# Expert choice for four tiles at a time, its links put one by one between the statistics of the attention loop

## Chip, core, metric

One core of a Trainium2 chip. The metric is the device time of one execution in microseconds (us); of the kernel before there are three timed runs and one profiled execution. The engines are called as the profile calls them: PE (TensorE, with PEld for its weight loads), DVE (VectorE), ACT (ScalarE), POOL (GpSimd), SP (the DMA queue of SyncE).

## What is computed

A gated cross-attention block and a gated mixture of experts over 64 sequences of 64 tokens with 128 features: 4096 tokens, all float32.

```python
x = x + tanh(g_xattn) * attention(layernorm(x), ctx)     # 16 heads of 64, q and k normalised by head
h = layernorm(x)
logits = h @ Wg;  probs = softmax(logits)                # 8 experts
vals, idx = top_k(probs, 2);  weights = vals / (sum(vals) + 1e-9)
expert e: silu(h @ W1[e] + b1[e]) @ W2[e] + b2[e]        # hidden width 512, for its tokens only
x = x + tanh(g_ffn) * (weighted sum of the two experts + 0.1 * (silu(h @ Ws1 + bs1) @ Ws2 + bs2))
```

Of two experts with the same logit the one with the lower number counts as the first.

## The kernel before

The 4096 tokens are 32 tiles of 128 (one per partition). Each engine runs a program of its own, written out by hand, and the engines meet at semaphores; the order of a program is the order in which its engine works, and an instruction whose wait isn't over holds up all behind it.

**The attention loop.** `steps` runs s from -5 to 31. A step works on several tiles at once: projections of tile s+2 and s+3, scores and softmax of tile s, the attention output of tile s-1, its residual and second layer norm (s-2, s-3), and the expert logits of tile s-4, which `keep_logits` (L889) copies to `lg_all`. DVE's step (L990) is in this order: `sum_squares` of q, `scale` of k, `row_sums` and `row_inverses` of the softmax, `residual` (L823, which PE waits for before it transposes the second half of k), two more `scale` and the other `sum_squares`, `normalise` (L883), then the statistics: `token_statistics` (bn_stats L813, bn_aggr L817) and `second_statistics` (L830, L832); then `maximum` (L855, when PE has done the scores) and `less_maximum_of` (L862), which PE waits for before it computes the logits (L1319) and the values, and ACT before the exponentials of the softmax; at the end `route_ranks`, `keep_logits` and `route`.

**Expert choice.** The tiles are routed BT = 8 at a time, in NB = 4 batches. The choice is a chain of small DVE instructions, each of which needs the result of the one before: `after` makes each of them count up `f_step` and then waits for that count. In the loop batch b starts 11 steps behind its first tile (`ROUTE_LAG`); five steps of eight carry a piece of it at the end of DVE's step: `less_highest` and `first_choice` (6 instructions), `highest_of_rest` and `second_choice` (6), `take_ranks` and `place` (4), `denominators` (3), `weigh` (3). ACT adds two small exponentials. PE counts the chosen experts with `ranks` (L1324 and L1326, 1 + BT small matmuls), and `take_ranks` (L929, L931) adds the running counts, so that `place` (L937) gives each token two rows (`slot`) of the array `routed` in HBM. Batches 0 to 2 are routed in steps 11 to 15, 19 to 23 and 27 to 31. Batch 3 comes behind the loop.

**Scatter.** POOL writes each tile's rows to `routed` by two indirect DMAs (L704), in the loop for the tile SCATTER_LAG = 15 steps back, so that tiles 0 to 17 go out in the loop and 14 tiles behind it.

**Behind the loop.** The last tile's attention is finished between transposes of the normed tokens (`transpose_tokens`, L1342), DVE's `lo_part` (L976) and the shared expert of five groups of four tiles (`shared_hidden` L1358 to L1360, `shared_result` L1374, `shared_out` L1043 and L1045). DVE also routes batch 3, then computes from the counts the schedule of the experts' work (L1074 to L1116). SP waits for the schedule and for all scatters before it loads rows of `routed` (L365). Then 40 work items run through the experts (`row_transpose` L1463, `row_hidden` L1475 to L1477, `row_out` L1491, results scattered by POOL at L763). At the end three more groups of the shared expert run while the experts' results come back: `shared_out` for groups 5 to 7 (L1039) and `combine` (L1168, L1172), which adds the two weighted expert rows to the tokens of group g, once ACT has weighted the second of them (L590).

## Time and profile before

| | us |
|---|---|
| median of 3 timed runs | 600.97 (599.75 to 601.02) |
| the profiled execution, device time | 599.88 |
| its span, first to last instruction | 597.7 |
| PE busy in the span | 567.4 (95%) |
| DVE busy | 454.2 (76%) |
| ACT busy | 453.3 (76%) |
| POOL busy | 359.9 (60%) |

The rows further down are of the profiled execution; times in them count from the start of its span, which is 2.2 us shorter than its device time. "Busy" of PE is not PE at its peak, since matmuls are pipelined. A row by stretch gives the window, its length, each engine's busy us with its instructions, TensorE's granted clock (1.00 is full), the DMA share and GB/s. A timeline row gives start, duration, engine, line and operation, and in brackets how long the engine had been idle and who ended that.

### The profile page before, as it was taken

The numbers are of one execution on the slowest core, as the hardware profiler recorded it, in microseconds if no ns is written. First come the engines' busy times: TensorE is split into PE (matmuls) and PEld (weight loads), VectorE is DVE, ScalarE is ACT, GpSimd is POOL, SyncE is SP. The second block draws the span as 40 slices with busy tenths as digits, with TensorE's granted clock in tenths as the row PEclk, the third lists the DMA queues.
The fourth block names the chain that finished last, engine by engine and source line by source line (L and its number), as shares of the span: only waits on it lengthen the run. The fifth ranks groups of instructions, "written<-read, shape, count | busy, mean of one in ns | idle before, by whom it ended". The sixth has DMA issues, their size and how long they took to land.

```text
span 597.7 us, 21071 instructions
## 1 busy us (share of the span) xinstructions
PE 567.4 (95%) x7675; PEld 508.0 (85%) x7675; DVE 454.2 (76%) x1048; ACT 453.3 (76%) x991; POOL 359.9 (60%) x709
## 2 busy tenths in 40 slices
PE   6989999999999999999999999889989999999993
PEld 5868888888888888878888888678889999999983
DVE  4689889889898988998998899755766554555637
ACT  3689999999888999888999988666445565565574
POOL 2545656756557787777778866757716555555410
PEclk9999999999999999999999999999999999999997
DMA  6910100120100101110020000001312222222155
GB/s 216 334 42 3 36 4 21 37 83 3 54 3 13 49 25 39 43 32 11 22 64 12 21 13 10 20 29 42 125 51 77 85 74 77 86 76 65 45 223 212
DMA packets 22500, 37.07 MB, mean 62 GB/s; under 512 B 5136, under 2 KB 13072, under 8 KB 22272
## 3 DMA queue, kind: packets, MB, share of 16 engines
q1 hardware_dynamic: 17792, 26.81, 14.2%
q0 software_dynamic: 4320, 8.92, 4.2%
q8 instruction: 63, 1.03, 0.7%
q14 instruction: 37, 0.30, 0.2%
q10 hardware_dynamic: 288, 0.00, 0.0%
HBM read 22.71 MB, written 13.01 MB: 60 GB/s over the span
## 4 chain that ended last, share of the span: by engine, by line
PE 76%; DVE 13%; issue 5%; ACT 2%; POOL 2%; DMA 2%; ACTq 0%; DVEq 0%; SPq 0%; POOLq 0%
PE ps L1491 10%; PE ps L1237 8%; PE ps L1205 7%; PE ps L1293 7%; PE ps L1207 6%; PE ps L1206 6%; PE ps L1263 6%; PE ps L1246 5%; PE ps L1278 4%; PE ps L1475 3%; PE ps L1476 3%; PE ps L1477 3%; PE ps L1374 2%; DVE wide L847 2%; DVE sm L869 2%
## 5 line engine op out<-in xcount | busy, mean ns | idle before, releaser
L763 POOL DMA_INDIRECT results<-spo,xs_ix x71 | 69.1, 973 | 69.3 <-DVE spo L1161 59.6
L439 ACT ACTIVATE qk_T<-ps,lnw 128x512 f32<-128x512 f32 x128 | 96.9, 786 | 6.8 <-PE ps L1237 6.2
L847 DVE TENSOR_TENSOR wide<-ps,rstd 128x512 f32<-128x512 f32 x128 | 87.1, 680 | 5.0 <-POOL rstd L678 5.0
L1205 PE MATMUL ps<-w_hi,xc_hi 128*128 128x512 f32 x192 | 87.1, 454 | 3.9 <-DVE w_lo L783 2.8
L840 DVE TENSOR_REDUCE ss<-wide 128x16 f32<-128x1024 f32 x64 | 77.8, 1216 | 15.4 <-ACT wide L415 14.0
L1237 PE MATMUL ps<-ident,wide 128*128 128x128 f32 x512 | 78.4, 278 | 4.0 <-ACT row_T L491 2.5
L415 ACT ACTIVATE wide<-ps 128x512 f32<-128x512 f32 x128 | 76.1, 596 | 2.2 <-PE ps L1207 2.2
L1237 PEld LDWEIGHTS ps<-ident,wide 128*128 128x128 f32 x512 | 58.9, 144 | 20.5 <-ACT spo L469 6.5
L1207 PE MATMUL ps<-w_hi,xc_lo 128*128 128x512 f32 x192 | 76.2, 397 | 0.0
L704 POOL DMA_INDIRECT routed<-rows_all,slot x64 | 65.4, 1021 | 17.5 <-issue 16.3
L1206 PE MATMUL ps<-w_lo,xc_hi 128*128 128x512 f32 x192 | 75.6, 394 | 0.0
L572 ACT ACTIVATE qk_T<-ps,b_now 128x256 f32<-128x256 f32 (+1 forms) x160 | 59.7, 451 | 17.7 <-PE ps L1477 15.8
L1491 PE MATMUL ps<-w_sb,qk_T 128*128 x568 | 70.3, 276 | 0.0
L1491 PEld LDWEIGHTS ps<-w_sb,qk_T 128*128 128x128 f32 x568 | 66.9, 192 | 0.1
L684 POOL TENSOR_TENSOR prob<-prob,rinv 128x1024 f32<-128x1024 f32 x32 | 60.9, 1904 | 9.7 <-DVE rinv L876 9.6
L1293 PE MATMUL ps<-wu_sb,spo 128*128 128x128 f32 x512 | 62.5, 275 | 0.1
L1293 PEld LDWEIGHTS ps<-wu_sb,spo 128*128 128x128 f32 x512 | 59.8, 192 | 3.3 <-ACT qk_T L439 0.4
L855 DVE TENSOR_REDUCE mx<-ps 128x8 f32<-128x512 f32 x64 | 41.2, 686 | 16.9 <-PE ps L1263 16.9
L1161 DVE TENSOR_TENSOR spo<-ps,b_all 128x256 f32<-128x256 f32 (+1 forms) x40 | 15.8, 396 | 46.9 <-PE ps L1491 46.9
L469 ACT ACTIVATE spo<-ps 128x512 f32<-128x512 f32 x64 | 34.9, 596 | 20.0 <-PE ps L1278 20.0
L1475 PE MATMUL ps<-w_lo,w_hi 128*128 128x256 f32 (+1 forms) x160 | 47.8, 299 | 1.2 <-DVE w_lo L1124 1.2
L1477 PE MATMUL ps<-w_lo,w_hi 128*128 128x256 f32 (+1 forms) x160 | 44.9, 280 | 0.0
(202 smaller groups left out, 1354.3 us busy)
## 6 DMA issues: line engine op xcount, KB each, us to landing
v_sb<-routed SPq DMA_DIRECT2D x31, 130.0 KB
xc_in<-in_x SPq DMA_DIRECT2D x8, 256.0 KB, 2.9
xc_in<-in_ctx SPq DMA_DIRECT2D x8, 256.0 KB, 4.7
w_raw<-in_L_ffn_W SPq DMA_DIRECT2D x8, 256.0 KB, 2.7
out_x<-x_res SPq DMA_DIRECT2D x8, 256.0 KB, 2.0
x_res<-in_x SPq DMA_DIRECT2D x1, 1792.0 KB, 8.6
w_raw<-results SPq DMA_DIRECT2D x3, 512.0 KB, 4.6
rows_all<-results SPq DMA_DIRECT2D x3, 512.0 KB, 8.6
```

Of the source, the lines that this page charges most:

```text
L415: nc.scalar.activation(sq[:, n, j * 512:j * 512 + 512], ps[2 * n + j][:, :], ACT.Square, scale=HD ** -0.5).then_inc(sq_ready[n][j], 1)
L439: nc.scalar.activation(qk_T[:, n, 4 * j:4 * j + 4, :].rearrange("p a n -> p (a n)"), ps[6 + j][:, :], ACT.Identity, bias=lnw[:, 2 * n + 1: ...
L763: gp_.indirect_dma_start(out=results[:, :], out_offset=bass.IndirectOffsetOnAxis(ap=xs_ix[:, b4, a:a + 1], axis=0), in_=yb[:, b4, a, :], i ...
L840: nc.vector.tensor_reduce(ss[:, n, :], sq[:, n, :].rearrange("p (h d) -> p h d", h=HEADS), AX.X, ALU.add).then_inc(ss_ready[n], 1)
L847: nc.vector.tensor_tensor(qk_n[:, n, j * 512:(j + 1) * 512].rearrange("p (h d) -> p h d", h=8), ps[2 * n + j][:, :].rearrange("p (h d) -> ...
L1205: nc.tensor.matmul(out_bank, xc_hi[:, t % XD, src, :], w_hi[:, w, cols[j]], start=True, stop=False)
L1206: nc.tensor.matmul(out_bank, xc_hi[:, t % XD, src, :], w_lo[:, w, cols[j]], start=False, stop=False)
L1207: return nc.tensor.matmul(out_bank, xc_lo[:, t % XD, src, :], w_hi[:, w, cols[j]], start=False, stop=True)
L1237: last = nc.tensor.transpose(ps[6 + j][:, a * P:(a + 1) * P], qk_n[:, n, c0:c0 + P], ident[:, :])
L1293: last = nc.tensor.matmul(ps[7][:, 0:D], o_T[:, p, :, :].rearrange("p b n -> p (b n)"), wu_sb[:, p, :], start=(p == 0), stop=(p == PAIRS - 1))
L1475: nc.tensor.matmul(h, w_hi_c, xs_hi[:, n % 2, cols_n], start=True, stop=False)
L1491: last_ = nc.tensor.matmul(ps[4 + n % 2][:, a * D:(a + 1) * D], hT[:, n % 2, c, a * P:(a + 1) * P], w2e[:, c, :], start=(c == 0), stop=(c ...
```

## The change

- BT becomes 4, so there are 8 batches. Six of them (0 to 5) are routed in the loop, batch b in the four steps from 4b + 8 (`ROUTE_LAG` 8): there is a batch at work in every step from 8 to 31. Batches 6 and 7 come behind the loop.
- Each link of the chain is a function of its own, and the wait for the link before stands in front of it (`last`), no longer behind the link it follows. `choose(s, piece)` gives DVE five links a step, one at each of five places: in front of `token_sums`, between it and `token_moments`, behind that, between `second_sums` and `second_moments`, and behind that; `token_statistics` and `second_statistics` are cut in two for it. Nothing of the choice but `take_ranks` is left at the end of DVE's step. ACT's small exponentials come one step later in the batch than before.
- The weights of a batch (`inverse`, `first_weight`, `second_weight`) are computed in the next batch.
- Behind the loop DVE gets, between the work that it had there: `divide(5)`, `choose_first(6)` before `lo_part(0)`, `choose_second(6)` before `residual(30)`, `place(6)` behind `lo_part(1)`, `weigh(6)` before `residual(31)`; batch 7 stands where batch 3 stood. PE counts batch 6 between the two halves of `shared_hidden(0)`, and waits for `take_ranks(6)` before the logits of tile 29.
- SCATTER_LAG becomes 13: tiles 0 to 19 go out in the loop, 12 tiles behind it.
- `combine(0)` stands in front of `shared_out(5)`.

The core of the diff (left out: helpers of the same kind as those shown):

```diff
@@ -27,7 +27,7 @@
 GN = GT * P
 EARLY = 5
 ROW = D + 2
-BT = 8
+BT = 4
 NB = TILES // BT
 XD = 4
 RT = 256
...
@@ -235,8 +235,8 @@
         block = stack.enter_context(nc.Block())
 
         LAST = TILES - 1
-        SCATTER_LAG = 15
-        ROUTE_LAG = 11
+        SCATTER_LAG = 13
+        ROUTE_LAG = 8
         RANKS_AT = 2
         PADS_AT, SPARES_AT, SPARES_SENT_AT, SPARES_DONE_AT = 7, 8, 9, 15
 
@@ -264,7 +264,7 @@
 
         def batch_at(s, lag):
             b, at = divmod(s - lag, BT)
-            return (b, at) if 0 <= b < NB - 1 else (None, 0)
+            return (b, at) if 0 <= b < NB - 2 else (None, 0)
 
         def r_slot(n):
             return n % 4, 16 * (n // 4 + 1)
...
@@ -500,9 +500,9 @@
 
             def route(s, lag):
                 b, at = batch_at(s, lag)
-                if b is not None and at == 0:
+                if b is not None and at == 1:
                     expert_exponentials(b)
-                if b is not None and at == 1:
+                if b is not None and at == 2:
                     second_exponentials(b)
 
...
             hi_part(1)
+            expert_exponentials(NB - 2)
             probabilities(0, LAST)
             probabilities(1, LAST)
+            second_exponentials(NB - 2)
             sc.preload_act_table_set("silu_and_others")
...
-            def token_statistics(t):
+            def token_sums(t):
...
+
+            def token_moments(t):
+                if has(t):
                     ve.wait_ge(bn_done, t + 1)
...
-            def second_statistics(t):
+            def second_sums(t):
...
+            def second_moments(t):
+                if has(t):
                     ve.wait_ge(bn2_done, t + 1)
...
-            choice = [0]
-
-            def after(ins):
-                choice[0] += 1
+            links = [0]
+
+            def last():
+                ve.wait_ge(f_step, links[0])
+
+            def link_of(ins):
+                links[0] += 1
                 ins.then_inc(f_step, 1)
-                ve.wait_ge(f_step, choice[0])
 
             def by_expert(a):
                 return a.unsqueeze(2).to_broadcast([P, BT, E])
 
             first_of = first_e[:, :].unsqueeze(1).to_broadcast([P, BT, E])
+
+            def logits_of(b):
+                return lg_all[:, BT * b:BT * b + BT, :]
+
+            def first_at(b):
+                return rows_all[:, BT * b:BT * b + BT, D + 1]
+
+            def highest(b):
+                ve.wait_ge(lg_ready, BT * (b + 1))
+                link_of(nc.vector.tensor_reduce(gm, logits_of(b), AX.X, ALU.max))
+
             def less_highest(b):
-                ve.wait_ge(lg_ready, BT * (b + 1))
-                lg = lg_all[:, BT * b:BT * b + BT, :]
-                after(nc.vector.tensor_reduce(gm, lg, AX.X, ALU.max))
-                nc.vector.tensor_tensor(gp, lg, by_expert(gm), ALU.subtract).then_inc(f_sub, 1)
+                last()
+                nc.vector.tensor_tensor(gp, logits_of(b), by_expert(gm), ALU.subtract).then_inc(f_sub, 1)
+
+            def ties(b):
                 ve.wait_ge(f_sub, b + 1)
-                after(nc.vector.scalar_tensor_tensor(tie, gp, 0.0, first_of, ALU.is_equal, ALU.mult))
+                link_of(nc.vector.scalar_tensor_tensor(tie, gp, 0.0, first_of, ALU.is_equal, ALU.mult))
+
+            def first_expert(b):
+                last()
+                link_of(nc.vector.tensor_reduce(first_at(b), tie, AX.X, ALU.max))
 
...
+            def others(b):
+                last()
+                link_of(nc.vector.scalar_tensor_tensor(rest, oh[:, 0, :, :], -3.0e38, gp, ALU.mult, ALU.add))
 
             def highest_of_rest(b):
+                last()
                 nc.vector.tensor_reduce(top, rest, AX.X, ALU.max).then_inc(f_top, 1)
...
+            def both_choices(b):
+                last()
                 nc.vector.tensor_tensor(picked[:, 0:BT, :], oh[:, 0, :, :], oh[:, 1, :, :], ALU.add).then_inc(f_cnt, 1)
...
+            def hits(b):
                 ve.wait_ge(f_taken, 2 * b + 2)
-                after(nc.vector.tensor_tensor(hit, oh, rank.unsqueeze(1).to_broadcast([P, 2, BT, E]), ALU.mult))
+                link_of(nc.vector.tensor_tensor(hit, oh, rank.unsqueeze(1).to_broadcast([P, 2, BT, E]), ALU.mult))
+
+            def slots(b):
+                last()
                 with nc.allow_low_precision("slots are whole numbers"):
                     nc.vector.tensor_reduce(slot[:, b, :, :], hit, AX.X, ALU.add).then_inc(f_slot, 1)
 
...
+            def choose(s, piece):
+                b, at = batch_at(s, ROUTE_LAG)
                 if b is None:
                     return
                 if at == 0:
-                    less_highest(b)
-                    first_choice(b)
+                    if piece == 0:
+                        highest(b)
+                    if piece == 1:
+                        less_highest(b)
+                    if piece == 2:
+                        ties(b)
+                    if piece == 3:
+                        first_expert(b)
+                    if piece == 4:
+                        first_choice(b)
                 if at == 1:
-                    highest_of_rest(b)
-                    second_choice(b)
-                if at == RANKS_AT:
-                    place(b)
+                    if piece == 0:
+                        others(b)
+                    if piece == 1:
+                        highest_of_rest(b)
+                    if piece == 2:
+                        equal_of_rest(b)
+                    if piece == 3:
+                        ties_of_rest(b)
+                    if piece == 4:
+                        second_expert(b)
+                if at == 2:
+                    if piece == 0:
+                        second_choice(b)
+                    if piece == 1:
+                        both_choices(b)
+                    if piece == 2 and b >= 1:
+                        inverse(b - 1)
+                    if piece == 3 and b >= 1:
+                        first_weight(b - 1)
+                    if piece == 4 and b >= 1:
+                        second_weight(b - 1)
                 if at == 3:
-                    denominators(b)
-                if at == 4:
-                    weigh(b)
+                    if piece == 0:
+                        hits(b)
+                    if piece == 1:
+                        slots(b)
+                    if piece == 2:
+                        gate_sum(b)
+                    if piece == 3:
+                        denominator(b)
+                    if piece == 4:
+                        with_second(b)
...
-                token_statistics(s + 3)
-                second_statistics(s - 2)
+                choose(s, 0)
+                token_sums(s + 3)
+                choose(s, 1)
+                token_moments(s + 3)
+                choose(s, 2)
+                second_sums(s - 2)
+                choose(s, 3)
+                second_moments(s - 2)
+                choose(s, 4)
                 maximum(1, s)
                 maximum(0, s)
                 less_maximum_of(1, s)
@@ -1008,23 +1102,61 @@
                 less_maximum_of(0, s)
                 route_ranks(s, ROUTE_LAG)
                 keep_logits(s - 4)
-                route(s, ROUTE_LAG)
             steps(step)
...
+            def choose_first(b):
+                highest(b)
+                less_highest(b)
+                ties(b)
+                first_expert(b)
+                first_choice(b)
+                others(b)
+
+            def choose_second(b):
+                highest_of_rest(b)
+                equal_of_rest(b)
+                ties_of_rest(b)
+                second_expert(b)
+                second_choice(b)
+                both_choices(b)
+
+            def place(b):
+                take_ranks(b)
+                hits(b)
+                slots(b)
+
+            def divide(b):
+                inverse(b)
+                first_weight(b)
+                second_weight(b)
+
+            def weigh(b):
+                gate_sum(b)
+                denominator(b)
+                with_second(b)
+                divide(b)
+
             normalise(LAST - 2)
+            divide(NB - 3)
             row_sums(LAST)
             row_inverses(LAST)
+            choose_first(NB - 2)
             lo_part(0)
             keep_logits(LAST - 3)
+            choose_second(NB - 2)
             residual(LAST - 1)
-            second_statistics(LAST - 1)
+            second_sums(LAST - 1)
+            second_moments(LAST - 1)
             lo_part(1)
+            place(NB - 2)
             nc.vector.tensor_scalar(tg01[:, :], tg[:, 1:2], SHARED, None, ALU.mult).then_inc(run0, 1)
...
             normalise(LAST - 1)
+            weigh(NB - 2)
             residual(LAST)
-            second_statistics(LAST)
+            second_sums(LAST)
+            second_moments(LAST)
...
-            less_highest(NB - 1)
-            first_choice(NB - 1)
-            highest_of_rest(NB - 1)
-            second_choice(NB - 1)
+            choose_first(NB - 1)
+            choose_second(NB - 1)
             lo_part(2)
-            take_ranks(NB - 1)
             place(NB - 1)
             shared_out(0)
-            denominators(NB - 1)
             weigh(NB - 1)
...
+            combine(0)
             shared_out(EARLY)
-            combine(0)
...
+                    if t == LAST - 2:
+                        pe.wait_ge(f_taken, 2 * (NB - 1))
...
             shared_hidden(0, range(2))
+            ranks(NB - 2)
             attend(LAST)
```

## Rows read from the trace of the kernel before

**Rows 1.** Busy us of PE, PEld, DVE, ACT, POOL; stretches: steps 11-16, 17-18, 19-24, 27-29.
```profile
154.71:224.83 70.12, 68.98 (x1147) 59.12 (x1149) 64.09 (x138) 63.12 (x135) 48.22 (x110) 1.00 0.09 31
224.83:247.12 22.29, 22.29 (x383) 19.66 (x386) 19.88 (x40) 20.69 (x45) 17.70 (x39) 1.00 0.10 26
247.12:317.74 70.62, 69.19 (x1147) 59.35 (x1150) 64.01 (x138) 63.00 (x135) 53.36 (x115) 1.00 0.12 37
340.07:376.03 35.96, 34.27 (x577) 28.96 (x580) 32.72 (x73) 30.64 (x65) 25.04 (x55) 1.00 0.05 14
```

**Rows 2.** The chain of waits in step 19, where DVE hands back to PE.
```profile
256.16 0.28 DVE x_res L823
...
256.49 0.66 PE ps L1237 x4
```

**Rows 3.** Timeline of DVE and PE in step 17, a step without choice.
```profile
224.53 0.34 DVE L883 TENSOR_SCALAR rows_all<-x_res,mv,rstd 128x128 f32<-128x128 f32 x1
224.79 0.28 DVE L813 BATCH_NORM_STATS2 bn<-x_res 128x6 f32<-128x128 f32 x1
225.11 0.18 DVE L817 BATCH_NORM_AGGREGATE mv<-bn 128x2 f32<-128x6 f32 x1
225.99 1.29 DVE L855 TENSOR_REDUCE mx<-ps 128x8 f32<-128x512 f32 x2 [0.30 <-PE ps L1263]
227.20 0.68 DVE L862 TENSOR_TENSOR prob<-ps,mx 128x512 f32<-128x512 f32 x1
228.06 0.29 PE L1319 MATMUL ps<-wg_raw,row_T 128*128 128x8 f32 x2
232.22 0.32 DVE L823 SCALAR_TENSOR_TENSOR x_res<-ps,tg,x_res 128x128 f32<-128x128 f32 x1
233.12 0.60 PE L1237 MATMUL ps<-ident,wide 128*128 128x128 f32 x4
233.95 1.22 DVE L840 TENSOR_REDUCE ss<-wide 128x16 f32<-128x1024 f32 x1 [0.82 <-ACT wide L415]
```

**Rows 4.** The chain of waits in step 21: a gap, and PE's count.
```profile
273.65 0.36 issue
...
275.81 0.05 PE ps L1324
275.86 0.19 PE ps L1326 x8
```

**Rows 5.** Timeline of DVE in step 13: two instructions that need nothing of each other.
```profile
183.25 0.21 DVE L929 TENSOR_TENSOR w_raw<-ps,base 128x64 f32<-128x64 f32 x1
183.38 0.15 DVE L931 TENSOR_TENSOR base<-ps,base 128x8 f32<-128x8 f32 x1
```

**Rows 6.** Timeline behind the loop: batch 3's choice on DVE, and PE behind it.
```profile
407.22 0.22 DVE L905 TENSOR_REDUCE w_raw<-lg_all 128x8 f32<-128x64 f32 x1
...
410.33 0.68 DVE L976 TENSOR_TENSOR w_lo<-ps,w_lo 128x512 fp32r<-128x512 f32 x1
...
411.16 0.63 PE L1342 MATMUL ps<-ident,rows_all 128*128 128x128 f32 x4 [0.58 <-DVE w_lo L976]
```

**Rows 7.** Timeline behind the loop: the last tile's probabilities and residual 30.
```profile
393.33 0.25 DVE L876 RECIPROCAL rinv<-sm 128x16 f32<-128x16 f32 x1
...
394.69 0.34 DVE L823 SCALAR_TENSOR_TENSOR x_res<-ps,tg,x_res 128x128 f32<-128x128 f32 x1
...
395.71 1.07 PE L1246 MATMUL ps<-ident,prob 128*128 128x128 f32 x8 [0.24 <-POOL prob L684]
```

**Rows 8.** Timeline of POOL, SP and PE: the last batch's scatters, row loads, first expert matmul.
```profile
413.27 0.95 POOL L704 DMA_INDIRECT routed<-rows_all,slot  x1 [1.17 <-DVE slot L937]
...
436.07 13.47 SPq L365 DMA_DIRECT2D v_sb<-routed  x6
...
441.07 0.39 PE L1475 MATMUL ps<-w_lo,w_hi 128*128 128x256 f32 x1 [1.16 <-DVE w_lo L1124]
```

**Rows 9.** Timeline of DVE near the end: `shared_out` of group 6.
```profile
584.88 0.75 DVE L1039 SCALAR_TENSOR_TENSOR x_res<-ps,tg,x_res 128x512 f32<-128x512 f32 x1 [0.30 <-PE ps L1374]
```

49 lines of the change are left out of this document (29 added, 20 removed).

## The prediction

> **What bounds the kernel now.** I read the views in this order. The page's busy shares (PE 95%, the others 60 to 76%) say only where to look. The busy time by stretch says what a step costs and which steps differ. In steps 17 and 18, which carry no choice, PE is busy for all of the 22.29 us, at the full granted clock: a step is 11.15 us of PE's work, and DVE has 19.88 of 22.29 busy [rows 1]. The three stretches with choice are longer: steps 11 to 16 take 70.12 us where six plain ones take 66.87, steps 19 to 24 take 70.62 for 66.87, steps 27 to 29 take 35.96 for 33.44. That is 3.25 + 3.75 + 2.52 = 9.5 us of excess, with PE idle for 1.14, 1.43 and 1.69 us of it and stretched matmuls for the rest [rows 1]. The chain of waits says who does it: in step 19 it leaves PE, runs down DVE through the choice, and comes back only when `residual` has read the output (L823 to PE's transposes at L1237) [rows 2]. So in these steps DVE is the bound, in the others PE.
>
> The timeline of a plain step says how much room DVE has. It idles twice: 0.30 us in front of `maximum`, waiting for the scores, and 0.82 us before the second sum of squares, waiting for ACT [rows 3]. Between the two it runs without a pause, so a delay of `maximum` is passed on. PE would feel it at two points. The residual is through at 232.54 and PE transposes the second half of k at 233.12, 0.6 us of slack. The logits start at 228.06, when `less_maximum_of` ended at 227.88: some 0.1 us of slack, which is all there is [rows 3].
>
> **The loop, what goes.** In the old place, the end of DVE's step, the choice stands between `less_maximum_of` and `residual` and has only the residual's 0.6 us of slack to hide in. Six links take 1.56 us there: in the same form behind the loop 12 links run from 407.22 to 410.33, 0.26 us a link [rows 6]. So a step with six links has to be about 1 us longer, and six such steps are 6 of the 9.5. From the excess of 9.5 I take what the change doesn't touch. PE's count is 0.05 + 0.19 us for each of three batches [rows 4], 0.72. In step 21 there is a gap of 0.36 us on PE in which it waits for nothing that the profile shows, with slower matmuls behind it [rows 4]; I leave 0.6 for it. 9.5 - 0.7 - 0.6 = 8.2 us go, if the new place is free.
>
> **The loop, what comes.** Five links a step in steps 8 to 31, 24 steps. No row shows a link of four tiles; from both sides: the instructions on 64 elements take 0.21 to 0.23 us and those on 8 take 0.15 [rows 5, 6], so 32 elements take about 0.19. What a link costs DVE depends on whether it has to wait for its neighbour. The upper end is one that waits: 0.22 (0.19 and the 0.03 to 0.05 by which 0.26 exceeds 0.22). The lower end is one that doesn't: L931 starts 0.13 us behind L929, which takes 0.21 [rows 5], so the next instruction starts some 0.08 before the profile's end of the one before, and a link on 32 elements costs 0.10 to 0.11. The places are laid out so that neighbours are never links: I go through one step. `normalise` gives way after 0.26 (224.53 to 224.79). Link 0 at 0.26, `token_sums` at 0.36, link 1 at 0.56, `token_moments` at 0.68, because it waits for its sums 0.32 us either way (224.79 to 225.11, [rows 3]); link 1 lies in that wait and costs nothing. Link 2 at 0.78, `second_sums` at 0.88, link 3 at 1.08 in the second such wait, `second_moments` at 1.20, link 4 at 1.30, DVE free at 1.40. `maximum` now starts at 1.46 (225.99 - 224.53), for the scores. So the five links fit into the two waits and the 0.30. In the step with `hits` (64 elements) it is 1.45, and the two or three instructions on 4 elements in the other steps are shorter. The middle is zero a step; I book 0.02 us for it, 0.5 us in all, since a margin of 0.05 isn't a margin. Bounds: 0 and, with every link at 0.22, see the rival below.
>
> PE's count: 1 + 4 small matmuls for six batches. By 0.19/8 us each and 0.05 that is 0.15, six times 0.9, for 0.72 now: +0.2. Below nothing it can't go, as the instructions grow in number. `take_ranks` stays where it is, twice as often, two instructions of 0.13 and 0.08: 3 more times 0.2 us, in the slack of 0.6 and of 0.82. ACT's exponentials come in 12 steps, at 0.2 us; they now need nothing of the same step. ACT is busy 20.69 of 22.29 us in two steps [rows 1], and what it delays, DVE's next `scale`, stands in front of the 0.82 us [rows 3]. Cost nothing; with that cover gone it would be 0.2 us in 12 steps.
>
> POOL: four more scatters in the loop, in steps 13 and 14, where it is as little loaded as in the stretch's mean, 48.22 of 70.12 us busy [rows 1]. What is queued behind a scatter on POOL is the next tile's reciprocal root, and a tile's slots are ready two steps before its scatter. Nothing.
>
> **Behind the loop.** `divide(5)` takes the place of the three instructions of the old `weigh`, during ACT's exponential. Then it costs: `choose_first(6)` starts behind `row_inverses`, 0.17 us after 393.33. Six links at 0.22 are 1.3, then `lo_part(0)` 0.6, `keep_logits` 0.1, `choose_second(6)` 1.2, and the residual of tile 30 starts at about 396.6 in place of 394.69 and is through at 396.95. PE's transposes of the second half of the last probabilities wait for it; they stand in the group that starts at 395.71, whose second half comes at about 396.24, half of its 1.07 us later [rows 7]. PE is 0.7 us late, with PE's count of batch 6 0.85; with links at 0.26 it would be 1.3. `place(6)` and `weigh(6)` lie beside PE's shared expert. What comes back: batch 7's twelve links take 12 x 0.22 = 2.65 in place of 3.11 us, and PE now waits 0.58 us for the `lo_part` behind them [rows 6], so all of 0.45 counts, and the count is 0.1 shorter. 0.85 - 0.45 - 0.1 = +0.3 us, bounds -0.1 and +1.0.
>
> The scatters: 12 tiles in place of 14 are left over, four scatters fewer, and the 1.17 us that POOL waited for the slots of batch 3 goes, since batch 6 is placed early. Sixteen scatters and the landing lie between 413.27 and 436.07 [rows 8], 1.43 us each at most; so SP can load rows 5 to 7 us sooner. This buys nothing by itself: the rows are there, PE's first matmul of the experts at 441.07 waits for DVE's `row_lo` (L1124) [rows 8], which stands behind the last `shared_out` and `lo_part`, and these behind PE's shared expert. The rows' transposes are late by at most a microsecond less than that. If they were the bound after all, it would be a gain of up to 1 us.
>
> **Near the end.** `combine(0)` moves into time in which DVE waits for PE's group 5; DVE is then ready some 0.4 us sooner for `shared_out(6)`, and there it waits for PE already now, 0.30 us [rows 9]. The gain is eaten: 0. It could be negative if ACT's weighting were late; PE needs `shared_out(5)` only for group 7, microseconds later.
>
> **The sum,** against the profiled execution's 599.88 us (span 597.7 and 2.2 around it): -8.2 + 0.5 + 0.2 + 0.3 = -7.2, so 592.7. That execution lies 1.1 below the median of the runs, 600.97, from which the same sum gives 593.8. I say 593.3.
>
> **A rule against it.** L931 starts while L929, by the profile, has 0.08 us to go [rows 5], and on this the links at 0.10 us rest. The Trainium skill, VectorE: DVE Perf Modes, The DRAIN you can't avoid, states that the next DVE operation doesn't start until the pipe of the last is empty and that leaving the semaphore out saves nothing; its Rules for kernel authors say to minimise the number of operations, not of semaphores. By it some 60 more small instructions in the loop (six batches of 22 less three of them, for three of 22) each cost their whole duration, which is the first rival's mechanism and its 609. The trace disagrees with the rule's strong form, by 0.13 against 0.26 us.
>
> **Rivals.** (1) Slower: a link costs its full 0.22 us wherever it stands, because DVE starts it only when its neighbour is done. Five are 1.1 us in front of `maximum`; 0.30 of idle time and 0.1 of slack before PE's logits cover 0.4, and PE is 0.7 us late in each of 24 steps: +16.8. With -8.2 + 0.5 for count and tail that is +9.1, 609. It decides from 0.32 us a step, where 24 of them eat 7.7. For it: the margin is so narrow, and waits stand in front of nearly every link. Against it: rows 5. Chance 0.07. (2) The gaps are only half used: a link costs 0.13 and each one between sums and moments pushes these by 0.05, so that `maximum` is late by 0.15 to 0.3 and PE by 0.05 to 0.25 a step: 1.2 to 6 us back, 594.5 to 599, typically 596.5. Chance 0.22. (3) It doesn't do what it says, since the excess has another cause than the choice (PE's code, POOL's scatters from step 15 on): against it speaks that steps 17 and 18, with scatters, are plain [rows 1]; 600. Chance 0.04. (4) More: the gap of step 21 was the choice's too, DVE gains margin and the rows' loads counted: 590 to 591.5. Chance 0.07.
>
> **Numbers.** The forecast, 591.5 to 595, has 0.60. The range for 8 in 10 takes in the fourth and most of the second: 590.5 to 598.8. What this kernel's measurement can tell from no change is about 0.2%, 1.2 us. Faster than that: 0.60 + 0.07 + 0.21 = 0.88; within it 0.05; slower 0.07.
>
> **What the profile after would show.** Right: steps 8 to 29 all at 11.15 to 11.35 us with PE busy throughout; links in front of `maximum` 0.10 to 0.15 us apart from their neighbours, and `maximum` still waiting for PE, if for 0.05 us. Wrong: `maximum` starting with no idle time before it, PE idle before L1319 or the values. Behind the loop PE idle for 0.7 us before the last probabilities' second half, the scatters ending over 5 us ahead of the first row's work, and `shared_out(6)` waiting 0.7 us. It is wrong as a whole if plain steps become longer than 11.4 us.

## The result, and the profile after

The changed kernel takes 597.81 us (median, 595.34 to 599.53) where the kernel before takes 601.02 (599.75 to 602.15): a ratio of 0.9941, 95% interval 0.9925 to 0.9957. The forecast was 593.3 us, a gain of 7.7 with a range of 590.5 to 598.8; it gained 3.2. The profiled execution took 597.49 us (span 595.7) beside 599.88 (span 597.7) before. Tables below speak of the *tail*: from the start of the last tile's scores on PE to the first matmul of the experts. A *gap* is a stretch in which PE stands still though the profile shows nothing that it waits for ("issue").

The first view is busy time by stretch, for the same steps as [rows 1] (columns as there).

```profile
155.65:222.72 67.07, 67.07 (x1141) 59.13 (x1140) 62.12 (x147) 62.36 (x135) 52.47 (x114) 1.00 0.12 36
222.72:245.15 22.43, 22.43 (x385) 19.77 (x384) 20.81 (x51) 20.93 (x47) 17.76 (x39) 1.00 0.08 26
245.15:314.87 69.72, 67.58 (x1141) 59.51 (x1140) 62.48 (x147) 62.58 (x135) 53.38 (x115) 1.00 0.11 37
338.21:371.27 33.06, 32.93 (x565) 28.84 (x564) 30.49 (x70) 30.09 (x64) 25.10 (x55) 1.00 0.05 15
```

Steps 11 to 16 went from 70.12 to 67.07 us and steps 27 to 29 from 35.96 to 33.06, PE busy in all of the first and all but 0.13 of the last: the choice no longer holds PE up. Steps 19 to 24 are only 0.9 us shorter, and PE is idle there for 2.14 us. The chain of waits says in what (start us, us, what):

```profile
269.89 0.82 PE ps L1406 x52
270.70 1.10 issue
271.81 0.45 PE ps L1406 x12
```

In the midst of `attend`'s 64x64 matmuls PE stands still with nothing to wait for. It is the gap of [rows 4], 0.36 us there, in this execution 1.10 in step 21, 1.04 in step 19, 0.94 in step 1 and 0.63 in step 25. Step 30 has one of 1.06, where the kernel before has 0.98; this one is in PE's timeline, but not on the chain of waits.

The timeline of DVE in step 17 answers [rows 3] (start us, us, line, operation, operands, idle time before it):

```profile
222.47 0.34 DVE L891 TENSOR_SCALAR rows_all<-x_res,mv,rstd 128x128 f32<-128x128 f32 x1
222.73 0.18 DVE L941 SCALAR_TENSOR_TENSOR w_raw<-w_raw 128x32 f32<-128x32 f32 x1
222.83 0.28 DVE L815 BATCH_NORM_STATS2 bn<-x_res 128x6 f32<-128x128 f32 x1
...
223.25 0.18 DVE L949 TENSOR_TENSOR w_raw<-w_raw 128x32 f32<-128x32 f32 x1
223.34 0.29 DVE L835 BATCH_NORM_STATS2 bn<-x_res 128x6 f32<-128x128 f32 x1
...
223.66 0.18 DVE L840 BATCH_NORM_AGGREGATE mv<-bn 128x2 f32<-128x6 f32 x1
223.76 0.18 DVE L957 TENSOR_REDUCE w_raw<-w_raw 128x4 f32<-128x32 f32 x1
223.94 1.29 DVE L863 TENSOR_REDUCE mx<-ps 128x8 f32<-128x512 f32 x2
```

A link gives way to the neighbour behind it after 0.09 to 0.12 us, though it is written as lasting 0.18, and `maximum` starts 1.47 us behind `normalise`, 1.46 before. Its idle 0.30 us is used up to the last hundredth. Even so PE's scores remain what it waits for: in the steps from 8 to 29 it starts 0.04 to 0.07 us behind their end, with 0 to 0.04 us of idle time before it from step 11 on.

Behind the loop, where the changed order has the first half of batch 6's choice ahead of the tokens' lower part, the timeline (answers [rows 7]) reads:

```profile
389.06 0.19 DVE L925 TENSOR_TENSOR w_raw<-lg_all,w_raw 128x32 f32<-128x32 f32 x1
389.07 1.95 POOL L686 TENSOR_TENSOR prob<-prob,rinv 128x1024 f32<-128x1024 f32 x1 [3.02 <-DVE rinv L884]
...
389.29 1.77 DVE L929 SCALAR_TENSOR_TENSOR w_raw<-w_raw,first_e 128x32 f32<-128x32 f32 x1
...
391.73 0.68 DVE L1063 TENSOR_TENSOR w_lo<-ps,w_lo 128x512 fp32r<-128x512 f32 x1
...
392.55 1.09 PE L1472 MATMUL ps<-ident,rows_all 128*128 128x128 f32 x4 [3.68 <-DVE w_lo L1063]
...
393.43 1.91 PE L1374 MATMUL ps<-ident,prob 128*128 128x128 f32 x8
...
393.62 0.34 DVE L828 SCALAR_TENSOR_TENSOR x_res<-ps,tg,x_res 128x128 f32<-128x128 f32 x1
```

The link `ties`, 0.18 to 0.27 us everywhere else in this execution, takes 1.77, and ends at 391.06, when POOL's product of the probabilities ends (391.02). PE is idle for 3.68 us, and its transposes behind that take 1.91 us for eight where [rows 7] has 1.07. The windows show a reason (the clock is the third number from the end):

```profile
388.70:392.50 3.80, 0.17 (x2) 0.00 (x0) 3.60 (x10) 0.69 (x2) 3.27 (x3) 0.99 0.00 0
392.50:394.00 1.50, 1.45 (x7) 1.48 (x8) 1.29 (x7) 0.32 (x1) 1.06 (x2) 0.50 0.14 44
394.00:396.00 2.00, 2.00 (x10) 1.86 (x9) 1.05 (x3) 1.61 (x5) 1.13 (x3) 0.55 0.10 33
396.00:398.00 2.00, 2.00 (x72) 1.61 (x72) 0.76 (x5) 1.36 (x2) 1.62 (x2) 1.00 0.13 39
```

After 3.8 us with 0.17 busy PE's clock is at half, the 1.2 GHz level, and back at 1.00 in the stretch from 396. The tail is 56.90 us long where it was 53.94.

The last scatters and the row loads (answers [rows 8]; rows of POOL, SP and PE), and `shared_out` of group 6 (answers [rows 9]):

```profile
425.92 0.96 POOL L706 DMA_INDIRECT routed<-rows_all,slot  x1 [0.31 <-issue]
...
433.13 3.65 SPq L365 DMA_DIRECT2D v_sb<-routed  x4
...
439.39 0.39 PE L1606 MATMUL ps<-w_lo,w_hi 128*128 128x256 f32 x1 [1.16 <-DVE w_lo L1252]
...
582.87 0.75 DVE L1171 SCALAR_TENSOR_TENSOR x_res<-ps,tg,x_res 128x512 f32<-128x512 f32 x1 [0.55 <-PE ps L1504]
```

**Where the time is.** Differences of the two profiled executions, in us: up to step 11 +1.0 (step 1's gap); steps 11 to 29 without gaps -8.7; their gaps +3.0; step 30 +0.04; tail +2.96; from the first expert matmul to the end -0.3. The sum is -2.0, the difference of the spans. The two middle terms are worked out so. Steps 11 to 29 take 221.32 and 215.62. A step with a gap is set beside the same step of an execution without it: 0.57 goes from before (step 21: 12.08, and 11.51 in before_shift_b, below), and 1.29, 1.38 and 0.92 from after (steps 19, 21 and 25 at 12.44, 12.53 and 12.07 beside plain ones of 11.15). That leaves 220.75 and 212.03. A gap so costs a quarter of a microsecond more than its own row.

A second set of runs of the same kernel, after_again, was the reference for the others:

> The changed kernel as it is, once more, for a second profile on this chip. Theory A (gaps of 0.2 to 1.1 us on PE in the middle of the 64x64 matmuls belong to places in PE's program, and whether one opens varies from run to run): the profile shows the loop's plain steps at 11.15 us again, two to five gaps of PE in L1406, each where the count of PE's instructions modulo 256 is 184 to 190, but not all the same ones; time 595.5 to 599.5. Rival B (the gaps come from the links or the scatters of particular steps): they stand in steps 19, 21 and 25 again, with the same lengths. Both: ties of batch 6 behind the loop takes 1.7 to 1.9 us again, PE idles 3.7 us before the transposes of group 1 and its granted clock is 0.5 for some us behind that.

597.53 us; the tail is 56.96, with a clock of 0.94, 0.50 and 0.63 in the same stretches, and steps 19 and 21 take 12.10 and 12.82 us. Step 25 has no gap in it, and takes 11.17.

Two things thus ate the gain: the tail, and PE's gaps. The experiments take them one after the other. The kernels, with medians, ratios to the kernel before on the same chip, and the tail and the sum of PE's gaps of 0.1 us and more, in its whole timeline, of each one's single profile:

| kernel | median us | ratio [95%] | tail | gaps |
|---|---|---|---|---|
| before | 601.02 to 602.14 | 1 | 53.94 | 1.86 |
| after | 597.81 | 0.9941 [0.9925, 0.9957] | 56.90 | 4.78 |
| after_again (the same kernel) | 597.53 | 0.9931 [0.9909, 0.9952] | 56.96 | 4.47 |
| links_bunched | 605.84 | 1.0060 [1.0037, 1.0084] | 57.04 | 3.74 |
| first_before_sums | 595.47 (single) | - | 55.22 | 4.42 |
| tail_order | 595.04 | 0.9887 [0.9867, 0.9908] | 53.64 | 4.00 |
| tail_order_3 (the same) | 594.58 | 0.9881 [0.9850, 0.9911] | 53.60 | 5.01 |
| warm_in_gap | 597.42 | 0.9919 [0.9894, 0.9944] | 56.18 | 5.66 |
| product_halves_2 | 596.70 | 0.9922 [0.9900, 0.9944] | 57.60 | 5.07 |
| old_scatter_combine | 597.76 | 0.9941 [0.9921, 0.9961] | 57.96 | 5.16 |
| pe_shift | 598.30 | 0.9938 [0.9917, 0.9959] | 56.97 | 3.55 |
| tail_order_shift | 594.07 | 0.9859 [0.9832, 0.9886] | 55.18 | 4.27 |
| before_shift_2 | 602.11 | 1.0015 [1.0000, 1.0029] | 53.94 | 4.05 |
| before_shift_b | 602.43 | 1.0027 [1.0011, 1.0042] | 53.95 | 2.53 |

Three more runs, on a chip on which the kernel before takes 641.85 us, are not comparable with these: product_halves 629.03 us (0.9797 [0.9756, 0.9837]), tail_order_again 629.34 (0.9799 [0.9764, 0.9833]) and before_shift 641.43 (0.9994 [0.9970, 1.0017]). tail_order_again is tail_order once more, expected at 0.9875 to 0.990.

### The profile page after: what moved, and what is told of

Same layout as the page of the kernel before. It is cut to its first block, busy times and chain, and to the rows that moved or that the text cites. A ratio compares the mean times of both kernels' runs of the same rounds, so it can differ in the third digit from the quotient of the medians.

```text
span 595.7 us, 21173 instructions
## 1 busy us (share of the span) xinstructions
PE 563.5 (95%) x7679; PEld 508.9 (85%) x7679; DVE 456.9 (77%) x1136; ACT 452.8 (76%) x999; POOL 361.4 (61%) x709
## 3 DMA queue, kind: packets, MB, share of 16 engines
q8 instruction: 63, 1.03, 0.7%
## 4 chain that ended last, share of the span: by engine, by line
PE 83%; DVE 6%; issue 3%; POOL 3%; ACT 3%; DMA 1%; ACTq 0%; DVEq 0%; POOLq 0%
PE ps L1622 11%; PE ps L1365 9%; PE ps L1421 9%; PE ps L1333 8%; PE ps L1335 7%; PE ps L1334 7%; PE ps L1391 6%; PE ps L1406 5%; PE ps L1374 5%; PE ps L1606 3%; PE ps L1607 3%; PE ps L1608 3%; PE ps L1504 3%; PE ps L1594 1%; DMA gates<-in_g_ffn 1%
## 5 line engine op out<-in xcount | busy, mean ns | idle before, releaser
L706 POOL DMA_INDIRECT routed<-rows_all,slot x64 | 65.7, 1026 | 16.3 <-issue 16.0
L1606 PE MATMUL ps<-w_lo,w_hi 128*128 128x256 f32 (+1 forms) x160 | 47.8, 299 | 1.3 <-DVE w_lo L1252 1.2
L1333 PEld LDWEIGHTS ps<-w_hi,xc_hi 128*128 128x128 f32 x192 | 36.1, 188 | 11.1 <-DVE w_lo L785 3.4
```

Of the source, the lines that this page charges most:

```text
L706: gp_.indirect_dma_start(out=routed[:, :], out_offset=bass.IndirectOffsetOnAxis(ap=slot[:, t // BT, c, t % BT:t % BT + 1], axis=0), in_=ro ...
L1333: nc.tensor.matmul(out_bank, xc_hi[:, t % XD, src, :], w_hi[:, w, cols[j]], start=True, stop=False)
```

## Experiments

### Is a link cheap because it stands alone? (links_bunched)

The five links of a step stand together behind the statistics, instead of one between each two of them:

```diff
-                choose(s, 0)
                 token_sums(s + 3)
-                choose(s, 1)
                 token_moments(s + 3)
-                choose(s, 2)
                 second_sums(s - 2)
-                choose(s, 3)
                 second_moments(s - 2)
-                choose(s, 4)
+                for piece in range(5):
+                    choose(s, piece)
```

> The same five links a step, but all behind the second statistics, one after the other, in front of maximum. Theory of the prediction (a link behind its neighbour costs 0.22 us, one with other work between 0.10; PE has 0.1 us of slack before the logits): DVE reaches maximum 0.8 us later than the scores are done, steps 8 to 29 take 11.8 us in place of 11.15, time about 612. Rival (PE's slack is the residual's 0.6 us and more, the logits' wait is made up for within the step): 11.2 to 11.4 us a step, 600 or less.

Measured: 605.84 us, a ratio of 1.0060 [1.0037, 1.0084] to before and 1.4% above after. Its steps from 11 on that have no gap take 11.63 to 11.78 us. The timeline of its step 17:

```profile
226.52 0.34 DVE L891 TENSOR_SCALAR rows_all<-x_res,mv,rstd 128x128 f32<-128x128 f32 x1
...
227.61 0.16 DVE L941 SCALAR_TENSOR_TENSOR w_raw<-w_raw 128x32 f32<-128x32 f32 x1
...
228.25 0.19 DVE L953 TENSOR_TENSOR w_raw<-w_raw,first_e 128x32 f32<-128x32 f32 x1
228.47 0.19 DVE L957 TENSOR_REDUCE w_raw<-w_raw 128x4 f32<-128x32 f32 x1
228.57 1.28 DVE L863 TENSOR_REDUCE mx<-ps 128x8 f32<-128x512 f32 x2
...
230.51 0.39 PE L1446 MATMUL ps<-wg_raw,row_T 128*128 128x8 f32 x2 [0.30 <-DVE prob L870]
```

The same five links cost 0.22 each when each needs the one before, `maximum` starts 2.05 us behind `normalise` instead of 1.47, and PE waits ahead of the logits. So what the change does in the loop works only through the interleaving. The first rival's 0.22 was the right price of a link in a row of links; the fifth, for which `maximum` doesn't wait, costs 0.10. Four at 0.22 and one at 0.10, less the 0.4 us of idle time and slack, are 0.58 us a step, and some 0.55 were passed on. That is less than the 0.65 of the expectation, and so is the time, 605.84 for 612.

### What does the tail cost, and why? (tail_order, tail_order_3, first_before_sums)

tail_order keeps only the maximum and the subtraction of it ahead of the tokens' lower part, and spreads the other links behind it (here the first of the three places; `weigh` is spread in the same way and PE's `ranks` stand behind `attend(LAST)`):

```diff
-            choose_first(NB - 2)
+            highest(NB - 2)
+            less_highest(NB - 2)
             lo_part(0)
             keep_logits(LAST - 3)
-            choose_second(NB - 2)
             residual(LAST - 1)
             second_sums(LAST - 1)
             second_moments(LAST - 1)
+            ties(NB - 2)
+            first_expert(NB - 2)
             lo_part(1)
-            place(NB - 2)
+            first_choice(NB - 2)
+            others(NB - 2)
+            choose_second(NB - 2)
...
```

> Behind the loop lo_part(0) and residual(30) go back in front of most of batch 6's links, ties(6) stands behind the POOL instruction that it lay under, and PE's count of batch 6 moves behind the second half of the shared expert's first group. Theory (the links' place behind the loop, with ties stretched to 1.77 us beside POOL's 128x1024 product and PE's clock halved by the 3.68 us of idle time, lost 2.9 us): from the last scores to the first expert matmul it takes 53.4 to 54.2 us in place of 56.9; no window behind the loop with a granted clock of 0.5; time 3 us below the changed kernel, about 594.8, ratio 0.990 to the kernel before. Rival (the tail is bound by its work, 12 more tiles' links and counts, wherever they stand): still 56 to 57 us, time 597.5.

Measured: 595.04 us, and the tail is 53.64. DVE and PE of its timeline:

```profile
388.28 1.95 POOL L686 TENSOR_TENSOR prob<-prob,rinv 128x1024 f32<-128x1024 f32 x1 [3.03 <-DVE rinv L884]
...
388.46 0.69 DVE L1063 TENSOR_TENSOR w_lo<-ps,w_lo 128x512 fp32r<-128x512 f32 x1
...
389.14 0.34 DVE L828 SCALAR_TENSOR_TENSOR x_res<-ps,tg,x_res 128x128 f32<-128x128 f32 x1
389.30 0.63 PE L1480 MATMUL ps<-ident,rows_all 128*128 128x128 f32 x4 [1.22 <-DVE w_lo L1063]
...
389.94 0.33 DVE L929 SCALAR_TENSOR_TENSOR w_raw<-w_raw,first_e 128x32 f32<-128x32 f32 x1
```

Beside the same product the instructions that take one operand from PSUM (L1063, L828) run at their usual length, and `ties`, 0.29 us before the product's end, takes 0.33: until that end. PE waits 1.22 us instead of 3.68 and keeps its full clock. So the tail's 3 us are the order's, and are given back. The same kernel once more:

> The same kernel as tail_order. Theory: 594.3 to 595.5, ratio 0.987 to 0.990, tail 53.6. Rival (its first result was the pauses' chance): 596.5 to 597.5.

594.58 us, tail 53.60: again.

first_before_sums puts the links of `choose_first` ahead of the sums and inverses of the last probabilities, that is, before POOL's product can start:

```diff
+            choose_first(NB - 2)
             row_sums(LAST)
             row_inverses(LAST)
-            choose_first(NB - 2)
             lo_part(0)
```

> choose_first(6) moves in front of row_sums(31), so that its six links run before POOL's product of the probabilities starts. Theory (DVE instructions with two SBUF inputs wait while POOL's product holds the SBUF port): ties(6) takes 0.19 us; the links that now fall beside the product, equal_of_rest and ties_of_rest, are the ones that stretch, until its end; row_sums is 1.0 to 1.4 us later, PE idles about 2 us in place of 3.68 before the transposes of group 1. Rival (ties(6) is slow for its own form, or because of what the links before it write): 1.7 us again in the new place, and no other stretches.

```profile
389.56 1.90 POOL L686 TENSOR_TENSOR prob<-prob,rinv 128x1024 f32<-128x1024 f32 x1 [3.91 <-DVE rinv L884]
...
390.21 1.29 DVE L949 TENSOR_TENSOR w_raw<-w_raw 128x32 f32<-128x32 f32 x1
...
391.54 0.38 DVE L953 TENSOR_TENSOR w_raw<-w_raw,first_e 128x32 f32<-128x32 f32 x1
```

`ties` is short now, and another link, the comparison at L949, has the stretch: 390.21 + 1.29 = 391.50, the product's end 391.46. The next, L953, takes 0.38. It is not the instruction but its place beside POOL's. The lower part is no longer behind it, PE waits 1.69 us for it, and the tail is 55.22.

### Does it end with POOL's instruction? (product_halves)

POOL's last product is issued as two instructions of half the size, which compute the same:

```diff
+                    if t == LAST:
+                        h = PAIRS
+                        nc.gpsimd.tensor_tensor(pv[:, 0:h, :], pv[:, 0:h, :], rinv[:, 0:h].unsqueeze(2).to_broadcast([P, h, S]), ALU.mult)
+                        nc.gpsimd.tensor_tensor(pv[:, h:, :], pv[:, h:, :], rinv[:, h:].unsqueeze(2).to_broadcast([P, h, S]), ALU.mult).then_inc(p_ready, 1)
+                        return
```

> The changed kernel, with GpSimd's last product (the probabilities of residual 31 by their inverse sums, 128x1024, 1.95 us in one instruction) issued as two instructions of 128x512. Computes the same. Theory A (a VectorE link that reads two operands of SBUF stands still until the GpSimd tensor_tensor that runs beside it has ended: the ties began at 389.29 and ended at 391.06, the product ran from 389.07 to 391.02): now the ties end with the first half, some 0.8 us long instead of 1.77, and the next two-operand link (w_raw less rows_all, L937 of the changed kernel) stands still for the second half, some 0.5 to 0.9 us instead of 0.19. The tokens' lower part is then ready within 0.3 us of before, the tail stays at 56.5 to 57.2 us and the time at that of the changed kernel, 597 to 598. Theory B (only the one long instruction starves VectorE at its start, and whoever comes after it is not touched): the ties take about 0.8 and no other link is stretched, the lower part comes 0.9 us sooner, TensorE's wait is 2.8 instead of 3.68, and the tail 55.2 to 56. Theory C (the stretch has nothing to do with GpSimd's product): the ties take 1.77 as before.

This run, before_shift and tail_order_again are the three on the chip at 641.85 us. In their profiles PE pauses for 0.2 to 0.5 us within the scores of nearly every step from 12 or 14 on; why isn't shown, and their times tell nothing of a few us. DVE's durations are the same there as in the run below, of the same kernel on a chip like the others:

> The same kernel as product_halves, in which the stretch of the ties fell to 0.92 us and the next two-operand link took 0.74, each until its half of the product had ended, so that the lower part is no sooner. Theory: time and tail of the changed kernel: 597 to 598, tail 56.4 to 57.2. Rival (the halves let the link between them through and save time): tail 55.5 to 56.2, 596 to 597.

```profile
388.35 1.09 POOL L688 TENSOR_TENSOR prob<-prob,rinv 128x512 f32<-128x512 f32 x1 [3.03 <-DVE rinv L889]
...
388.56 0.92 DVE L934 SCALAR_TENSOR_TENSOR w_raw<-w_raw,first_e 128x32 f32<-128x32 f32 x1
389.40 1.04 POOL L689 TENSOR_TENSOR prob<-prob,rinv 128x512 f32<-128x512 f32 x1
389.51 0.19 DVE L938 TENSOR_REDUCE rows_all<-w_raw 128x4 f32<-128x32 f32 x1
389.74 0.74 DVE L942 TENSOR_TENSOR w_raw<-w_raw,rows_all 128x32 f32<-128x32 f32 x1
390.39 0.45 POOL L697 TENSOR_TENSOR x_res<-x_res,tgbu 128x128 f32<-128x128 f32 x1
390.51 0.38 DVE L946 SCALAR_TENSOR_TENSOR w_raw<-w_raw 128x32 f32<-128x32 f32 x1
```

Theory A, by its mechanism: `ties` ends at 389.48, 0.04 behind the first half; the reduction, with one tensor as input, is untouched; the next two-tensor link ends at 390.48, 0.04 behind the second half; and the third at 390.89, 0.05 behind POOL's bias. Each waits for the POOL instruction, of these three, that is running when it wants to start. The sum is nearly as long as before, 0.73 + 0.55 + 0.19 us over the usual 0.19, and PE's wait is 3.50. The tail, 57.60, lies above the expected 56.4 to 57.2; PE's clock was 0.50 for longer, from 392 to 396. The time, 596.70, lies where the rival had it (596 to 597), with a tail that speaks against the rival; it can't be told from after's.

The Trainium skill, SBUF — State Buffer, section "SBUF: two separate sides", states this as a rule: VectorE with two inputs in SBUF and a GpSimd operation that reads SBUF use one shared pair of ports, whoever starts first has it for its whole instruction, and the other is fully blocked. The runs agree for POOL's products and its addition of the bias: all seven two-tensor links shown at over 0.3 us, here, in the section before and in the result, wait for POOL's end, and none with an operand in PSUM does. They don't show it for every POOL instruction. Beside a scatter (L706) the loop's links nearly keep their length: L949 in step 17, at 223.25, takes 0.18 us while a scatter runs from 222.67 to 223.64, and of 197 two-tensor links of 128x32 that lie within a scatter, in the ten profiles with interleaved links, 187 take at most 0.21 us and the others at most 0.27.

### What is PE's lower clock worth? (warm_in_gap)

Fifteen matmuls (30 in the trace) into a bank that is free then, with no use, ahead of the waiting transposes. This adds work that no output needs.

```diff
+            for _ in range(15):
+                nc.tensor.matmul(ps[0][:, 0:P], ident[:, :], ident[:, :], start=True, stop=True)
             transpose_tokens(1)
```

> The changed kernel with 15 matmuls of the identity (128x128, results not used) on PE where it idles 3.68 us, in front of the transposes of group 1. Theory (part of the loss behind the loop is TensorE's clock at its lower level after that idle time): the granted clock stays 1.00, the transposes of group 1 take 0.63 us in place of 1.09, those of the probabilities 1.1 to 1.4 in place of 1.91, and from the last scores to the first expert matmul it takes 55.4 to 56.0 us in place of 56.9; time about 1.2 us below the changed kernel. Rival (the residual and DVE's links hold PE anyway, the lower clock is hidden): 56.7 to 57.0, no change.

```profile
389.15 3.51 PE L1559 MATMUL ps<-ident 128*128 128x128 f32 x30
...
393.00 0.63 PE L1472 MATMUL ps<-ident,rows_all 128*128 128x128 f32 x4 [0.34 <-DVE w_lo L1063]
...
394.46 0.66 PE L1374 MATMUL ps<-ident,prob 128*128 128x128 f32 x4 [0.39 <-DVE x_res L828]
```

The clock stays at 1.00 and the tail is 56.18, 0.75 us shorter than the mean of after and after_again. The halved clock had made these transposes 0.46 and 0.65 us longer, but the second half of the last ones waits for the residual anyway. So of the tail's 3 us about 0.75 are the clock, and the rest is the wait for POOL's product and the forecast lateness. The time, 597.42, can't be told from after's.

The lower clock also spreads the tails: old_scatter_combine's is 1 us longer with the same waits, because its clock is 0.50 up to 398 and 0.83 to 400, and the shared expert's matmuls of 128x512 run at 0.43 us each in the chain of waits. In tail_order_shift it fell (0.61 and 0.54 from 391 to 395) with PE busy for 0.64 of the 2 us before, and that tail is 55.18; in tail_order and tail_order_3, with the same waits of 1.22 and 0.45 us, it didn't, and theirs are 53.6. So with these waits it falls in one execution and not in another.

### The scatters and the weighted sum (old_scatter_combine)

```diff
-        SCATTER_LAG = 13
+        SCATTER_LAG = 15
...
-            combine(0)
             shared_out(EARLY)
+            combine(0)
```

> Two parts of the change undone, the scatters 15 steps behind and combine(0) behind shared_out(5). Theory (both stand beside PE and DVE work that ends later): from the last scores to the first expert matmul 56.9 us as in the changed kernel, the last scatter some 5 us later but still ahead of need; the time from the last expert matmul to the end as in the changed kernel; time the same within 0.5 us. Rival (the scatters' earlier end is worth what it moved): 1 to 5 us slower than the changed kernel.

The time is that of after, 597.76. Its last scatter starts at 432.70 and not at 425.92, and PE's first expert matmul still waits 1.16 us for `row_lo`: the 6.8 us that POOL is sooner done buy nothing that can be seen.

### PE's gaps: who makes them? (pe_shift, before_shift, tail_order_shift)

Count all of PE's instructions in the trace: matmuls, weight loads, and those that its sequencer handles alone, waits for the most part (the counts in the expectations left some of these out, and so say 184 to 190). The gaps of before then stand at 4288, 5056, 8641 and 12224, those of after at 704, 7873, 8641, 10176 and 12224. Divided by 256 all of them leave 192 or 193, and so do all 76 gaps of 0.1 us and more in the fourteen profiles of the table. The page counts 63 packets of 1.03 MB together on the queue of kind "instruction", 16 KB each; PE's 7679 matmuls, as many weight loads and 948 others are 16,306 instructions, or 63.7 times 256. So there is a place in PE's program every 256 instructions, and a gap opens mostly when it falls into `attend`'s 64 matmuls of 64x64 (71 of the 76; the other five, of 0.12 to 0.56 us, are in transposes and projections). Ten more calls of a warming matmul at the very start, in time where PE waits for loads anyway, are 20 more matmuls in the trace (7699 for 7679) and shift all that follows by 40 instructions:

```diff
-            keep_warm(8)
+            keep_warm(18)
```

> The changed kernel with ten more warm-up matmuls (40 instructions) on PE before the first projection, in time in which it waits for DVE. Theory A (a gap of PE belongs to every 256th instruction of its program, when that one falls in the fast 64x64 matmuls): gaps again only where the count modulo 256 is 184 to 190, so 20 matmuls earlier in the work than before: the one that was at the 52nd matmul of L1406 in step 21 is now at the 32nd, shorter or gone, and others can open. Rival B (the gap of step 21, found in each profile so far with 0.4 to 1.4 us, belongs to what step 21 does): it stays at the 52nd matmul, 1.1 us. Time within 1.5 us of the changed kernel either way.

```profile
348.12 0.80 PE ps L1406 x50
348.91 1.40 issue
```

Step 21, which had its gap behind the 52nd matmul in every profile of the unshifted order (1.09 to 1.36 us), has none and takes 11.17 us; that of step 19 is at the 42nd in place of the 62nd and down to 0.13; steps 8, 10, 26, 28 and 30 have 0.33 to 1.40. All stand at 192 or 193. Where the gaps stand belongs to the place, and not to the order on DVE. Their sum is 3.55 us, less than the 4.78 and 4.47 of the two unshifted profiles, and yet the median is no lower, 598.3.

The same for the kernel before, by 10 and by 18 matmuls:

> The kernel before with keep_warm(18) for keep_warm(8) at its start (hidden time), once more, since before_shift ran beside a kernel before of 641.85 us, whose TensorE paused in nearly every residual. Theory A (a pause at one place in every 256 rows of TensorE's program, whoever stands there): the pauses move to other residuals (8, 16, 26 to 28), their sum is anything from 1 to 3.5 us. If the kernel before stood at a lucky place, the ratio is 1.002 to 1.004. Rival B (few pauses wherever the kernel before is put): sum below 1.6, ratio 0.999 to 1.001.

> The kernel before with keep_warm(26): 36 rows later in TensorE's program. Same theories as before_shift_2: A, the pauses stand at yet other residuals and add up to 1 to 3.5 us (if the places are a lottery, the mean of this and of before_shift_2 lies above the 1.55 of the kernel before, ratio 1.001 to 1.003); B, below 1.6 and ratio 0.999 to 1.001.

```profile
225.72 0.68 PE ps L1278 x43
226.40 0.88 issue
```

Gaps of 4.05 and 2.53 us where the kernel before has 1.86, all at 192 or 193, and times of 1.0015 and 1.0027 of it. (The first has them in steps 6, 8, 10, 19, 21, 28 and 30 and not only where I expected them, and its sum is above the expected 3.5.) So the kernel before stands at a lucky place, by 0.9 to 1.6 us if the ratios are taken at their middle (the first one's interval reaches down to 1). Whether the new order also opens more gaps at any place isn't separated: the ten profiles with interleaved links have 3.6 to 5.7 us, the three of the old order 1.9, 2.5 and 4.1. (before_shift, on the disturbed chip, gave 0.9994 [0.9970, 1.0017] and decides nothing.)

Last, both at once, the order of tail_order and the shift:

> The version with the links behind the loop in another order, and PE's program moved by 40 instructions as well. Theory A for the gaps: the plain steps, the tail (53.6 us from the last scores to the first expert matmul) and the end unchanged, the gaps of steps 19 and 21 moved 20 matmuls ahead or gone; time 593.5 to 595.5, in the same band as without the shift, lower by 1 us if the gaps close. Rival: gaps at the same places, 595.0.

594.07 us, a ratio of 0.9859 [0.9832, 0.9886]: the best of all kernels here, though its interval overlaps that of tail_order. I take the gain from the tail as shown and that from the shift as not.

The times of the instruction packets in the traces say what PE waits for. There is one packet of 16 KB for each place, and each of the 76 gaps ends 1.12 to 1.64 us behind the end of the packet before it: in step 19 of after the packet runs from 245.40 to 246.83, and PE stands still from 247.24 to 248.28. At 783 other places in the same profiles PE goes on without a gap, and passes none of them sooner than 1.10 us behind its packet. So the length of a gap, 0.11 us in one run and 1.49 in another, is how much too early PE reaches the place. The Trainium skill, Advanced Engine Details and Errata, section ISA Cache, states that a line of the instruction cache is 16 KB, 256 instructions; the period measured here is that. That a gap is PE waiting for the next line is read from these times and not from an experiment, since no run delayed a packet; why the packets come sooner or later stays open.

## Why the prediction was right or wrong

In the spans of the profiled executions the forecast of -7.2 us became -2.0: the loop gave 1.2 us more than forecast and the end 0.3 more, the gaps took 4.0 and the tail 2.7. By the medians 3.2 us came of 7.7.

**The loop, what goes and what comes: right in kind, 1.2 us too careful.** Forecast -8.2 + 0.5 + 0.2 = -7.5, measured without gaps -8.7. The 8.2 went as said. The links' 0.02 a step were nothing: `maximum` came 1.47 us behind `normalise` for a forecast of 1.40 to 1.46, where 1.46 was needed. PE's count is 0.11 to 0.15 us a step as forecast, and only four of its steps (14, 18, 22 and 26) lie between 11 and 29. The forecast's sign of failure, `maximum` with no idle time before it, is there (no row shows any from step 11 on), and meant nothing, since PE's scores still come last. And step 29 takes 10.77 us, 0.4 less than the 11.15 I had taken for every plain step; it has less of PE's work, since there is no tile 32 to project, which the choice had hidden.

**"In step 21 there is a gap of 0.36 us ...; I leave 0.6 for it": the first step that failed.** I took a gap that nothing explained as a constant of the kernel. It belongs to a place in PE's program, and its length is how much too early PE gets there (0.36 us before, 1.10 and 1.36 after, each time at the place with the count 8641). The gaps came to 3.0 us more in steps 11 to 29 and 1.0 in step 1, which no line of the change touches. Some 0.9 to 1.6 us of that is that the kernel before was lucky, by the two shifted ones; what the rest is, the new order or chance, stays open. The range for such a term, from the rows of one profile, was 0.2 to 1 us a gap and several gaps; I gave it none.

**"Six links at 0.22 are 1.3": the second.** The size was right for links on DVE alone and wrong beside POOL. Forecast for the tail +0.3, bounds -0.1 and +1.0; measured +2.96. The residual of tile 30 starts 11.13 us behind the last scores; before, it was 7.56 (394.69 in [rows 7], the scores at 387.13). I had forecast 1.9 us of the 3.6; 1.6 are the ties' wait for the product. That put PE's idle time at 3.68 us, its clock fell, and this added 0.75. I had listed whom POOL's queue keeps waiting, and hadn't asked what DVE does beside POOL's long product. The trace of before had an instance: the `normalise` of tile 28, six times its usual length, at 384.11, right behind the product's start at 384.10:

```profile
384.10 1.90 POOL L684 TENSOR_TENSOR prob<-prob,rinv 128x1024 f32<-128x1024 f32 x1 [1.54 <-DVE rinv L876]
384.11 1.97 DVE L883 TENSOR_SCALAR rows_all<-x_res,mv,rstd 128x128 f32<-128x128 f32 x1
```

0.34 us in [rows 3], 1.97 here. (It has one tensor as input; the same section of the Trainium skill names operations in a two-port mode beside those with two inputs. Whether this is one no run tests.) Earlier in the loop of before there are smaller ones: in four of ten steps with a scatter running, `normalise` takes 0.46 to 0.60 us and ends 0.02 to 0.03 behind it, in the other six its usual 0.34. Beside the product DVE has work from PSUM or a reduction in those steps. Behind the loop the old order was protected by having none of its links there.

**What came back behind the loop** was right: batch 7's twelve links take 2.58 us (406.16 to 408.74) for 3.11, -0.53 where -0.45 was forecast. The forecast sign that PE would be idle 0.7 us before the second half of the last probabilities is not to be seen; the 3.68 us ahead of them cover it.

**Scatters and the sum in front: right that they buy nothing, wrong in what stood behind the scatters.** POOL's last one starts 6.8 us sooner than in old_scatter_combine, but SP's row loads do not come 5 to 7 us sooner: 433.13 for 436.07 before is 2.9, and 435.85 in old_scatter_combine. The last scatter of after has landed at 428.70, so SP waits for something else by then; its own last writes of padding rows are issued until 428.89, and their landing is likely, not shown. `shared_out(6)` waits 0.55 us for PE (0.30 before, 0.7 forecast).

**The rule against the change** (links at full price, 609) did not come true, and links_bunched shows when it would: the trace disagrees with what the prediction took from the Trainium skill, VectorE: DVE Perf Modes, section "The DRAIN you can't avoid", that the next DVE operation doesn't start until the pipe of the last is empty, for neighbours that need nothing of each other, 0.10 us apart at a duration of 0.18, and agrees where each needs the one before, 0.22. The same section says itself, at the end of its first paragraph, that a next operation which isn't held starts earlier; I had quoted its stronger half only.

**The rivals.** By its time the result falls into the second's range (594.5 to 599), by its mechanism into none: `maximum` is not late. A rival "the tail pays" was missing, and so was one for the gaps, though both had a row in the trace of before.

## What to carry to other kernels

Small dependent steps on VectorE are nearly free when each stands between two instructions that need nothing of it, and cost twice as much in a row; here a margin of 0.05 us held in the 22 steps from 8 to 29. Before moving VectorE work with two operands in SBUF, look at what GpSimd runs beside the new place: beside a product or an addition of GpSimd's it stood still until that had ended (beside its scatters it hardly did), and what waits behind may cost TensorE its clock too. A pause that no wait explains is a term with a range of its own; shift the program by a few instructions on both kernels before crediting or blaming a change for a fraction of a per cent.
